# One window loop on one core: constants padded to 128 rows, masks turned in a strip bank, and another order of the TensorE blocks in a slot

## Chip, cores and metric

One NeuronCore of a Trainium2 chip runs the whole program. The metric is the device time of one execution in microseconds (us), taken on that core. The kernel before took 2175.47 us (median of 3 runs, 2175.24 to 2191.92).

## What is computed

For each of 128 batches of 128 nodes with 512 features, the reference makes a self feature, two directions of masked attention against the first 20 nodes with 16 heads, and adds both through a relu to the input:

```python
q_exp = jnp.where(row_zero[..., None], 0.0, q[:, None, :])
self_feat = jnp.concatenate([exp_v, q_exp], axis=-1) @ W_self.T + b_self
output = self_feat
for d in range(2):
    A = (adj_f if d == 0 else jnp.swapaxes(adj_f, 1, 2))[:, :, :20, :]
    qh = (self_feat @ Wq[d].T + bq[d]).reshape(B, N, 16, 32)
    kh = (self_feat[:, :20] @ Wk[d].T + bk[d]).reshape(B, 20, 16, 32)
    aff = einsum('bnhd,bmhd->bnhm', qh, kh) / sqrt(32)
    aff = where((A.sum(-1) > 0)[:, :, None, :], aff, NEG) + (A @ w_bias + b_bias)[:, :, None, :]
    w = softmax(aff)
    out_t = einsum('bnhm,bmf->bnhf', w, self_feat[:, :20])
    output = output + einsum('bnhf,hgf->bnhg', out_t, Wout[d]).reshape(B, N, F) + bout[d]
return exp_v + relu(output)
```

## The kernel before

The program has three stages. Weights are prepared, then keys and values of the 20 nodes of all batches are made and stored in DRAM (k_dram, v_dram), and from about 360 us on the window loop runs, which is where the change lies. It is written engine by engine, by hand: each engine executes its own list strictly in order, and semaphores tie the lists together. No scheduler moves anything.

The window loop works on pairs of batches, 64 of them, one new pair a slot. Slots 0 to 3 and the last ones are written out; the 14 rounds between run in a hardware loop of 4 slots. A pair stays in the window for 4 slots, at ages 0 to 3, and each slot makes one quarter of the scores of all 4 pairs in the window (one direction, 8 heads). In slot t, "soft" is the pair of age 3, whose scores become complete in this slot and whose softmax starts, "late" is the pair before it, "nxt" the pair that enters next. Two batches of a pair are b = 0 and 1.

The parts of a slot that matter here:

- generate(nxt, step), lines 1530 to 1548: makes the operand of the next slot's scores in four banks (low_banks), in 5 steps. Each step is 8 matmuls on strips of 32 rows, four of them side by side. Step 0 makes the constants from zl (line 1545), whose stationary operand has ZR = 41 columns; steps 1 to 4 make the keys (line 1547). All steps write the same columns, so each step waits until the one before it has been copied out. Step 0 is read twice: ScalarE copies it to zc (constants_high, line 1423), then VectorE forms the low part from the same bank (constants_low, line 1255), and step 1 waits for that (z_low). Steps 2 to 4 wait for ScalarE's keys_out (line 1428).
- scores(t, age), lines 1552 to 1569: per batch four float32 matmuls against kx (line 1567) and one fp32r matmul of 41 rows, flags against zc (line 1568), which adds the constants. A float32 matmul is two instructions in the trace, an fp32r matmul one. Two banks take turns, so scores wait for the add_masks of the scores two before (s_added).
- self_features (line 1580), 12 fp32r matmuls of 512 columns per batch into the bank OUT; values (line 1601) adds the attention output there. The next batch's self_features must wait until VectorE has taken OUT away (take_out, line 1294, out_taken).
- turn_weights (line 1593) turns a batch's softmax weights in the bank TURN, and ScalarE copies them out (weights_out, line 1441). TURN also takes flag_rows (line 1609, stationary 128 rows by 41 columns) and, every second slot, turn_mask (line 1615), the turned mask of a group of 4 batches.
- VectorE in a slot: add_masks(t,3) (line 1268), two maxima (line 1280), constants_low(nxt), add_masks(t,2), denominators of batch 0 (lines 1285, 1287), take_out(late,1), denominators of batch 1, add_masks(t,1), the turn of x, count_and_weigh of the edges, add_masks(t,0), total_and_mask, take_out(soft,0).
- GpSimd subtracts the maxima (shift, line 1358) and makes the normalised weights (line 1367); ScalarE makes the exponentials between them (line 1433).
- ScalarE in a slot: clip, high, constants_high(nxt), weights_out(late,1,0), high, exponentials(soft,0), weights_out(late,1,1), keys_out 0, exponentials(soft,1), clip(late,1), two scale_condition, row_sums, keys_out 1, the weights_out of soft's batch 0, and the rest. The masks are copied out of TURN to m1s (line 1460) and placed pair by pair (line 1471).

The order of a slot on TensorE is the code of slot(t):

```python
scores(t, 3); generate(nxt, 0); turn_weights(late, 1, 0)
scores(t, 2); turn_weights(late, 1, 1); generate(nxt, 1); values(late, 1)
scores(t, 1); generate(nxt, 2)
self_features(soft, 0, range(0, 2)); turn_weights(soft, 0, 0)
self_features(soft, 0, range(2, C)); turn_weights(soft, 0, 1)
generate(nxt, 3); scores(t, 0); flag_rows(nxt); values(soft, 0)
generate(nxt, 4); self_features(soft, 1, range(0, C))
# every second slot: turn_mask(g)
```

Of the kernel before, what the change touches and what calls it, by code (L numbers as in the profile page):

```python
# [893 lines left out]
def window_loop(nc, sb, sem, bank, low_banks, v):  # L894
# [28 lines left out]
    zl = sb("zl", [P, NO, ZR], F32)  # L923
    nzm = sb("nzm", [P, WIN, ZR], BF16)
# [11 lines left out]
    m1s = sb("m1s", [P, EDGE, NG], F32)  # L936
# [39 lines left out]
    m1_ready = sem("m1_ready")  # L976
# [19 lines left out]
    OUT, TURN = bank[6], bank[7]  # L996

# [190 lines left out]
    def vector_program(dve):  # L1188
# [18 lines left out]
        def nonzero_rows(p):  # L1207
# [6 lines left out]
            for o in (0, Q):  # L1214
                a = p.ring * (ZR + 1) + o
                nc.vector.tensor_scalar(spread[:, a:a + ZR + 2:ZR + 1], sums[:], 0.0, None,
                                        ALU.not_equal).then_inc(nz_ready, 1)
# [12 lines left out]
        def total_and_mask(g, d):  # L1230
# [6 lines left out]
            if d == 0:  # L1237

                if due(g):
                    dve.wait_ge(mask_set, 4 * g)  # L1240
# [16 lines left out]
        def add_masks(t, a):  # L1257
# [4 lines left out]
            if a == 0:  # L1262
# [3 lines left out]
                dve.wait_ge(mask_set, 2 * (p.n + 1))  # L1266
# [29 lines left out]
        def slot(t):  # L1296
# [28 lines left out]
            if has_edges(g):  # L1325
                count_and_weigh(g, t.c % 2)
            if t.real():
# [3 lines left out]
            if soft.real():  # L1331
                take_out(soft, 0)
# [64 lines left out]
    def scalar_program(act):  # L1397
# [53 lines left out]
        def flags_out(p):  # L1451
            act.wait_ge(pe_e, p.n + 1)
            nc.scalar.activation(flags[0:ZR, p.ring:p.ring + 2, :], TURN[0:ZR, 0:2 * N].rearrange("p (b n) -> p b n", b=2),
                                 ACT.Copy).then_inc(e_out, 1)

        def mask_out(g):
            if due(g):
                act.wait_ge(mask_set, 4 * g)
            act.wait_ge(pe_m1, g + 1)
            nc.scalar.activation(m1s[:].rearrange("p b m -> p (b m)"), TURN[:, 0:EDGE * NG], ACT.Copy).then_inc(m1_ready, 1)  # L1460

        def place_masks(t, p):

            g = edge_group(t.back(1) if p.c % 2 == 0 else t.back(2))
            o = 2 * (p.c % 2)
            if p.back(4).real():
                act.wait_ge(s_added, scored(t, 3))
            act.wait_ge(m_done[0], g + 1)
            act.wait_ge(m1_ready, g + 1)
            for d, m in enumerate((m0s, m1s)):  # L1470
                nc.scalar.activation(masks[:, d, p.ring:p.ring + 2, :], m[:, o:o + 2, :], ACT.Copy).then_inc(mask_set, 1)

        def slot(t):
# [12 lines left out]
            if t.c % 2 == 0 and nxt.real():  # L1486
                place_masks(t, nxt)
# [11 lines left out]
            if nxt.real():  # L1499
                row_sums(nxt)  # L1500
            if has_window(nxt):
# [199 lines left out]
```

## Time and profile before

| what | value |
|---|---|
| median of 3 runs | 2175.47 us |
| the profiled execution, its own time | 2179.28 us |
| its span in the trace | 2177.4 us |
| window loop, from its first matmul to the end | about 364 to 2177 us |
| one slot of the hardware loop | 26.4 to 27.0 us, the first of a round 26.6, 28.2 or once 30.8 us, the last of a round 28.6 to 30.6 us |
| busy share of TensorE, VectorE, ScalarE, GpSimd | 94%, 50%, 48%, 33% |

A row of the trace's groups gives line, engine, tiles, shapes, the count, the busy time and the mean, and behind the second bar the idle time just before and who ended it. PE is TensorE's matmul side, PEld its weight loads, DVE is VectorE, ACT ScalarE, POOL GpSimd, SP SyncE. A weight load that starts well ahead of its own matmul is hidden beside the matmul before; one that starts together with its matmul is not. In a timeline, rows of one line that follow each other are merged, so "1.25 ... x8" is eight matmuls from the first start to the last end; the last end overlaps the next start, and what a block occupies is best read from start to start.

### The profile page before, as it was taken

The numbers are of one execution on the slowest core, as the hardware profiler recorded it, in microseconds if no ns is written. First come the engines' busy times: TensorE is split into PE (matmuls) and PEld (weight loads), VectorE is DVE, ScalarE is ACT, GpSimd is POOL, SyncE is SP. The second block draws the span as 40 slices with busy tenths as digits, with TensorE's granted clock in tenths as the row PEclk, the third lists the DMA queues.
The fourth block names the chain that finished last, engine by engine and source line by source line (L and its number), as shares of the span: only waits on it lengthen the run. The fifth ranks groups of instructions, "written<-read, shape, count | busy, mean of one in ns | idle before, by whom it ended". The sixth has DMA issues, their size and how long they took to land. (4 is left out here: it accounts for less than half of the span.)

```text
span 2177.4 us, 47943 instructions
## 1 busy us (share of the span) xinstructions
PE 2047.9 (94%) x15864; PEld 1708.9 (78%) x15864; DVE 1096.0 (50%) x1937; ACT 1035.0 (48%) x1813; POOL 725.2 (33%) x617
## 2 busy tenths in 40 slices
PE   8999997799999999999999999999999999999997
PEld 5999996677777777777777777777777777777786
DVE  3433333455555555555555555555555545555532
ACT  3323232355455555555555555555555545455543
POOL 0323220033333333333333333333333333333334
PEclk9999998799999999999999999999999999999998
DMA  6132334444354435443444444444443444444322
GB/s 199 35 95 87 91 101 113 124 130 127 113 135 130 128 109 134 120 126 117 127 114 130 119 137 116 138 112 139 114 134 109 131 120 126 126 126 127 100 72 73
DMA packets 263777, 256.08 MB, mean 118 GB/s; under 512 B 78192, under 2 KB 194160, under 8 KB 263536
## 3 DMA queue, kind: packets, MB, share of 16 engines
q1 hardware_dynamic: 259072, 252.83, 41.5%
q8 instruction: 153, 2.51, 0.5%
q10 hardware_dynamic: 4464, 0.02, 0.1%
q14 instruction: 88, 0.72, 0.1%
HBM read 197.94 MB, written 54.79 MB: 116 GB/s over the span
## 5 line engine op out<-in xcount | busy, mean ns | idle before, releaser
L1567 PE MATMUL bank<-kx,xt_main 128*128 128x160 f32 x4096 | 691.2, 312 | 29.7 <-issue 29.4
L1567 PEld LDWEIGHTS bank<-kx,xt_main 128*128 128x128 f32 x4096 | 586.1, 193 | 73.5 <-issue 44.9
L1268 DVE TENSOR_TENSOR sc<-bank,masks 128x320 f32<-128x320 f32 x256 | 125.8, 492 | 712.8 <-PE bank L1568 712.8
L1376 POOL TENSOR_TENSOR res<-res,xk 128x512 f32<-128x512 f32 x128 | 163.5, 1277 | 879.5 <-ACT res L1418 879.5
L1428 ACT ACTIVATE kx<-low_banks 128x1280 f32<-128x1280 f32 (+3 forms) x268 | 317.9, 1186 | 182.8 <-PE low_banks L1547 182.7
L1580 PE MATMUL bank<-ws_h,xh_main 128*128 128x512 f32 x512 | 221.8, 433 | 52.4 <-DVE res L1294 52.3
L1547 PE MATMUL low_banks<-key_tile,a_rows 32*128 32x160 f32 (+3 forms) x4288 | 221.6, 321 | 17.6 <-DVE zc L1255 12.1
L1358 POOL TENSOR_TENSOR sc<-sc,mx 128x640 f32<-128x640 f32 x128 | 160.1, 1272 | 176.0 <-DVE mx L1280 175.9
L1423 ACT ACTIVATE zc<-low_banks 41x1280 fp32r<-41x1280 f32 (+2 forms) x67 | 79.3, 1184 | 265.3 <-PE low_banks L1545 265.3
L1580 PE MATMUL bank<-ws_h,xl_main 128*128 128x512 f32 x512 | 203.1, 397 | 0.0
L1580 PE MATMUL bank<-ws_l,xh_main 128*128 128x512 f32 x512 | 202.8, 396 | 0.0
L1547 PEld LDWEIGHTS low_banks<-key_tile,a_rows 32*128 32x128 f32 x4288 | 158.7, 188 | 54.3 <-issue 20.9
L1441 ACT ACTIVATE wtt<-bank 128x384 f32<-128x384 f32 (+1 forms) x256 | 110.9, 433 | 181.4 <-PE bank L1593 181.3
L1352 POOL TENSOR_TENSOR xl_main<-xt_main,xh_main 128x512 fp32r<-128x512 f32 x128 | 162.7, 1271 | 65.9 <-ACT xh_main L1407 65.9
L1601 PE MATMUL bank<-vbd,wtt 128*128 128x128 f32 x1280 | 177.7, 286 | 3.6 <-ACT wtt L1441 3.5
L1367 POOL TENSOR_TENSOR wt<-sc,rs 128x640 f32<-128x640 f32 x128 | 163.1, 1274 | 45.4 <-DVE rs L1287 45.4
L1568 PE MATMUL bank<-zc,flags 41*128 41x160 f32 x512 | 175.4, 343 | 0.0
L1601 PEld LDWEIGHTS bank<-vbd,wtt 128*128 128x128 f32 x1280 | 153.5, 192 | 21.1 <-ACT wtt L1441 9.6
L1580 PEld LDWEIGHTS bank<-ws_h,xh_main 128*128 128x128 f32 x512 | 96.4, 188 | 92.9 <-issue 70.8
L1568 PEld LDWEIGHTS bank<-zc,flags 41*128 41x128 f32 x512 | 94.6, 185 | 89.6 <-issue 89.6
L75 DVE STREAM_TRANSPOSE xt_main<-rows_main 128x256 f32<-128x256 f32 x256 | 141.6, 608 | 0.0
L1294 DVE TENSOR_TENSOR res<-bank,res 128x512 f32<-128x512 f32 x128 | 87.9, 687 | 83.6 <-PE bank L1601 83.6
(145 smaller groups left out, 3095.7 us busy)
## 6 DMA issues: line engine op xcount, KB each, us to landing
rows_main<-in_x SPq DMA_DIRECT2D x256, 128.0 KB, 4.6
xs<-in_x SPq DMA_DIRECT2D x64, 512.0 KB, 4.8
xk<-in_x SPq DMA_DIRECT2D x64, 512.0 KB, 3.9
res<-c_dram SPq DMA_DIRECT2D x64, 512.0 KB, 5.8
out<-res SPq DMA_DIRECT2D x128, 256.0 KB, 2.2
adj<-in_mask_BxSxSx_ik SPq DMA_DIRECT2D x32, 440.0 KB, 7.0
adj<-in_mask_BxSxSx_ik SPq DMA_DIRECT2D x128, 110.0 KB
vbd<-v_dram SPq DMA_DIRECT2D x768, 10.0 KB
```

What stands on the lines that cost most here:

```text
L75: return eng.transpose(dst, src.rearrange("p t (r j) -> p t r j", j=NQ)[:, :, :, j])
L1268: nc.vector.tensor_tensor(o[:, :, HU * hh:HU * hh + HU, d, :], s_bank(t, a).rearrange("p (b h m) -> p b h m", b=2, m=NG), masks[:, d, p.ri ...
L1352: pool.tensor_tensor(xl[:, :, b, :], xt[:, :, p.ring + b, :], xh[:, :, b, :].bitcast(F32), ALU.subtract).then_inc(x_low, 1)
L1358: pool.tensor_tensor(s, s, mx[:, b, :].unsqueeze(2).to_broadcast([P, DIRS * H, NG]), ALU.subtract).then_inc(s_shifted, 1)
L1367: pool.tensor_tensor(wt[:, b, :].rearrange("p (h m) -> p h m", m=NG), sc[:, p.ring + b, :].rearrange("p (h m) -> p h m", m=NG), rs[:, b, : ...
L1376: pool.tensor_tensor(res[:, p.par, b, :], res[:, p.par, b, :], xk[:, p.par, b, :], ALU.add).then_inc(res_ready, 1)
L1428: nc.scalar.activation(taken(kx[:, t.par, j], lo, hi), generated(0, P, lo, hi), ACT.Copy).then_inc(gen_taken, 1)
L1547: mm = nc.tensor.matmul(low_banks[:, r, dst], a_rows[s, o, step - 1, :], rhs, start=True, stop=True)
L1567: mm = nc.tensor.matmul(dst, xt[:, j, p.ring + b, :], kx[:, t.par, j, :, :, w, :].rearrange("p r c m -> p c r m"), start=(j == 0), stop=False)
L1568: mm = nc.tensor.matmul(dst, flags[0:ZR, p.ring + b, :], zc[0:ZR, t.par, :, :, w, :].rearrange("p r c m -> p c r m"), start=False, stop=True)
L1580: mm = nc.tensor.matmul(OUT[:], a, m[:, j, :], start=(j == 0 and k == 0), stop=False)
L1601: mm = nc.tensor.matmul(OUT[:, 3 * c * DH:(3 * c + SLOTS) * DH], wtt[:, b, c, :], vbd[:, p.par, c, :, b * DH:b * DH + DH], start=False, st ...
```

## The change

It has three parts.

First, padding: ZR is no longer used for zl, nzm, zc and flags in the window loop. They are 128 wide, zero beyond row 40, so that the constants' stationary operand has 32 rows by 128 columns, flag_rows 128 by 128, and the last matmul of each batch's scores 128 rows.

Second, masks: the turned mask of a group goes to unused columns of the first strip bank (MASK) instead of TURN, in the middle of an even slot. The copy m1s is gone; the masks are placed once a group for 4 batches, behind row_sums in ScalarE's list, and generate(nxt, 3) waits for that.

Third, order: TensorE's slot begins with generate(nxt, 0) and turn_weights(late, 1, 0), ahead of scores(t, 3); scores(t, 2) stands behind values(late, 1); scores(t, 0) stands behind values(soft, 0). VectorE's take_out(soft, 0) stands ahead of add_masks(t, 0). The rest of VectorE's list is as it was. Line numbers after the change are lower by 1 to 15.

```diff
-    zl = sb("zl", [P, NO, ZR], F32)
-    nzm = sb("nzm", [P, WIN, ZR], BF16)
+    zl = sb("zl", [P, NO, P], F32)
+    nzm = sb("nzm", [P, WIN, P], BF16)
...
+    MASK = low_banks[:, 0, 2 * UN:2 * UN + EDGE * NG]
...
             if d == 0:
 
                 if due(g):
-                    dve.wait_ge(mask_set, 4 * g)
+                    dve.wait_ge(mask_set, 2 * g)
...
-                dve.wait_ge(mask_set, 2 * (p.n + 1))
+                dve.wait_ge(mask_set, 2 * (p.half + 1))
...
                 count_and_weigh(g, t.c % 2)
+            if soft.real():
+                take_out(soft, 0)
             if t.real():
                 add_masks(t, 0)
             if has_edges(g):
                 total_and_mask(g, t.c % 2)
-            if soft.real():
-                take_out(soft, 0)
...
-            nc.scalar.activation(taken(zc[0:ZR, t.par], lo, hi), generated(0, ZR, lo, hi), ACT.Copy).then_inc(z_high, 1)
+            nc.scalar.activation(taken(zc[:, t.par], lo, hi), generated(0, P, lo, hi), ACT.Copy).then_inc(z_high, 1)
...
-        def place_masks(t, p):
...
+        def place_masks(t):
+
+            if t.back(3).real():
                 act.wait_ge(s_added, scored(t, 3))
-            act.wait_ge(m_done[0], g + 1)
-            act.wait_ge(m1_ready, g + 1)
-            for d, m in enumerate((m0s, m1s)):
-                nc.scalar.activation(masks[:, d, p.ring:p.ring + 2, :], m[:, o:o + 2, :], ACT.Copy).then_inc(mask_set, 1)
+            act.wait_ge(m_done[0], t.half + 1)
+            act.wait_ge(pe_gen, STEPS * (t.n + 1) + 3)
+            for d, m in enumerate((m0s[:], MASK.rearrange("p (b m) -> p b m", b=EDGE))):
+                nc.scalar.activation(masks[:, d, t.ring:t.ring + EDGE, :], m, ACT.Copy).then_inc(mask_set, 1)
...
-                        mm = nc.tensor.matmul(low_banks[0:ZR, r, dst], zl[s, o, :], rhs, start=True, stop=True)
+                        mm = nc.tensor.matmul(low_banks[:, r, dst], zl[s, o, :], rhs, start=True, stop=True)
...
-                mm = nc.tensor.matmul(dst, flags[0:ZR, p.ring + b, :], zc[0:ZR, t.par, :, :, w, :].rearrange("p r c m -> p c r m"), start=False, stop=True)
+                mm = nc.tensor.matmul(dst, flags[:, p.ring + b, :], zc[:, t.par, :, :, w, :].rearrange("p r c m -> p c r m"), start=False, stop=True)
...
-                mm = nc.tensor.matmul(TURN[0:ZR, b * N:b * N + N], nzm[:, p.ring + b, :], identity_b[:],
+                mm = nc.tensor.matmul(TURN[:, b * N:b * N + N], nzm[:, p.ring + b, :], identity_b[:],
...
-            if soft.real():
-                scores(t, 3)
             if has_window(nxt):
                 generate(nxt, 0)
             if late.real():
 
                 pe.wait_ge(e_out, t.n + 1 if t.real() else PAIRS)
-                g = edge_group(t.back(2) if t.c % 2 == 0 else t.back(3))
-                pe.wait_ge(m1_ready, g + 1 if has_edges(g) else EG)
                 turn_weights(late, 1, 0)
-            if t.back(2).real():
-                scores(t, 2)
+            if soft.real():
+                scores(t, 3)
             if late.real():
                 turn_weights(late, 1, 1)
             if has_window(nxt):
                 generate(nxt, 1)
             if late.real():
                 values(late, 1)
+            if t.back(2).real():
+                scores(t, 2)
             if t.back(1).real():
                 scores(t, 1)
+            if t.c % 2 == 0 and t.real():
+                turn_mask(t)
             if has_window(nxt):
                 generate(nxt, 2)
...
             if has_window(nxt):
+                if t.c % 2 == 0 and t.real():
+                    pe.wait_ge(mask_set, 2 * (t.half + 1))
                 generate(nxt, 3)
-            if t.real():
-                scores(t, 0)
...
             if soft.real():
                 values(soft, 0)
+            if t.real():
+                scores(t, 0)
             if has_window(nxt):
                 generate(nxt, 4)
             if soft.real():
                 self_features(soft, 1, range(0, C))
-            if t.c % 2 == 1:
-                g = edge_group(t.back(1))
-                if has_edges(g):
-                    if nxt.real():
-                        pe.wait_ge(e_out, nxt.n + 1)
-                    turn_mask(g)
```

On TensorE, in the first slot of the hardware loop, this stood from turn_weights(late, 1, 0) to the wait of generate(nxt, 1) before the change (z_low is raised by VectorE's constants_low; line 1567 and 1568 are scores(t, 2)):

```order
L1593 MATMUL bank<-identity,wt 128x128 [waits wt_ready,wtt_ready,m1_ready,e_out]
L1593 MATMUL bank<-identity,wt 128x128 x2
L1560 REGISTER_ALU
L1567 MATMUL bank<-kx,xt_main 128x160 [waits s_added]
L1567 MATMUL bank<-kx,xt_main 128x160 x3
L1568 MATMUL bank<-zc,flags 128x160
L1567 MATMUL bank<-kx,xt_main 128x160 x4
L1568 MATMUL bank<-zc,flags 128x160
L1588 REGISTER_ALU [waits wt_ready]
L1593 MATMUL bank<-identity,wt 128x128 [waits wtt_ready]
L1593 MATMUL bank<-identity,wt 128x128
L1547 MATMUL low_banks<-key_tile,a_rows 128x160 [waits z_low]
```

Scores(t, 3) had stood above generate(nxt, 0), so that the whole of scores(t, 2) lay between scores(t, 3) and the wait for z_low. In the changed kernel, from the end of scores(t, 3) on (lines 1552, 1553), the same stretch reads:

```order
L1552 MATMUL bank<-kx,xt_main 128x160 [waits gen_taken]
L1553 MATMUL bank<-zc,flags 128x160
L1552 MATMUL bank<-kx,xt_main 128x160 x4
L1553 MATMUL bank<-zc,flags 128x160
L1573 REGISTER_ALU [waits wt_ready]
L1578 MATMUL bank<-identity,wt 128x128 [waits wtt_ready]
L1578 MATMUL bank<-identity,wt 128x128
L1532 MATMUL low_banks<-key_tile,a_rows 128x160 [waits z_low]
L1532 MATMUL low_banks<-key_tile,a_rows 128x160 x7
L1584 REGISTER_ALU [waits vbd_loaded1]
L1586 MATMUL bank<-vbd,wtt 128x128 [waits wtt_ready]
L1586 MATMUL bank<-vbd,wtt 128x128 x4
```

Between scores(t, 3) and the wait for z_low now stand two transposes.

On VectorE the slot begins as it did: this is the changed kernel, and before it was the same with lines one higher (the ISA and REGISTER rows between carry no work):

```order
L1267 TENSOR_TENSOR sc<-bank,masks 128x2x8x20 [waits pe_s]
L1279 TENSOR_REDUCE mx<-sc 128x32 [waits s_added] x2
L1251 REGISTER_ALU
L1254 TENSOR_TENSOR zc<-low_banks,zc 9x1280 [waits z_high]
L1260 REGISTER_ALU
L1267 TENSOR_TENSOR sc<-bank,masks 128x2x8x20 [waits pe_s]
```

constants_low (line 1254) keeps its place behind add_masks of scores(t, 3) and both maxima. At the end of VectorE's slot, before the change:

```order
L1227 TENSOR_TENSOR adj<-adj,wb 128x880 [waits edge_sum]
L1261 REGISTER_ALU
L1268 TENSOR_TENSOR sc<-bank,masks 128x2x8x20 [waits mask_set,wt_ready,pe_s]
L1233 TENSOR_REDUCE vb<-adj 128x80 [waits weighed]
L1234 TENSOR_SCALAR mk<-cn 128x80
L1240 REGISTER_ALU [waits masked,bias_sum0]
L1247 SCALAR_TENSOR_TENSOR m0s<-vb,bb,mk 128x80 [waits mask_set]
L1294 TENSOR_TENSOR res<-bank,res 128x512 [waits pe_out,c_scaled]
```

and in the changed kernel, where take_out (line 1293) has moved ahead of add_masks and of the mask's arithmetic:

```order
L1226 TENSOR_TENSOR adj<-adj,wb 128x880 [waits edge_sum]
L1293 TENSOR_TENSOR res<-bank,res 128x512 [waits pe_out,c_scaled]
L1260 REGISTER_ALU
L1267 TENSOR_TENSOR sc<-bank,masks 128x2x8x20 [waits mask_set,wt_ready,pe_s]
L1232 TENSOR_REDUCE vb<-adj 128x80 [waits weighed]
L1233 TENSOR_SCALAR mk<-cn 128x80
L1246 SCALAR_TENSOR_TENSOR m0s<-vb,bb,mk 128x80 [waits mask_set,masked,bias_sum0]
```

TensorE's self_features(soft, 1) waits for that take_out, and in the changed kernel scores(t, 0) and generate(nxt, 4) stand between the values that it needs and that wait.

## Rows read from the trace of the kernel before

**Rows 1.** The page: busy time of each engine, share of the span, instructions.

```profile
PE 2047.9 (94%) x15864; PEld 1708.9 (78%) x15864; DVE 1096.0 (50%) x1937; ACT 1035.0 (48%) x1813; POOL 725.2 (33%) x617
```

**Rows 2.** Who waited for whom, whole span: total us, times, longest.

```profile
PEld bank L1568 <- issue: 89.6, 512, 0.3
...
PE bank L1580 <- DVE res L1294: 52.3, 65, 1.1
...
PE bank L1567 <- issue: 29.4, 13, 3.5
```

**Rows 3.** Timeline of the start of one slot (start us, length us, engine).

```profile
1034.82 1.24 PEld L1567 LDWEIGHTS bank<-kx,xt_main 128*128 128x128 f32 x8
1035.04 1.25 PE L1567 MATMUL bank<-kx,xt_main 128*128 128x160 f32 x8
...
1036.22 0.18 PEld L1568 LDWEIGHTS bank<-zc,flags 41*128 41x128 f32 x1 [0.17 <-issue]
1036.22 0.34 PE L1568 MATMUL bank<-zc,flags 41*128 41x160 f32 x1
...
1036.49 1.35 PE L1567 MATMUL bank<-kx,xt_main 128*128 128x160 f32 x8
...
1038.05 0.75 PE L1545 MATMUL low_banks<-key_tile,zl 32*41 32x160 f32 x16
1038.15 0.49 DVE L1268 TENSOR_TENSOR sc<-bank,masks 128x320 f32<-128x320 f32 x1 [6.14 <-PE bank L1568]
1038.68 1.54 DVE L1280 TENSOR_REDUCE mx<-sc 128x32 f32<-128x640 f32 x2
...
1039.58 2.50 POOL L1358 TENSOR_TENSOR sc<-sc,mx 128x640 f32<-128x640 f32 x2 [3.69 <-DVE mx L1280]
...
1040.25 1.48 DVE L1255 TENSOR_TENSOR zc<-low_banks,zc 9x1280 fp32r<-9x1280 f32 x1
...
1042.12 0.44 PE L1593 MATMUL bank<-identity,wt 128*128 128x128 f32 x2
...
1042.49 0.83 PE L1547 MATMUL low_banks<-key_tile,a_rows 32*128 32x160 f32 x16
```

**Rows 4.** The windows of that slot's four scores: sum of lengths, then PE busy.

```profile
sum 12.13, PE 12.13 PEld 10.06 DVE 5.55 ACT 6.53 POOL 5.50; mean PE 3.03 PEld 2.51 DVE 1.39 ACT 1.63 POOL 1.37
```

**Rows 5.** Timeline of the middle of that slot, one engine after the other.

```profile
1044.73 0.69 DVE L1294 TENSOR_TENSOR res<-bank,res 128x512 f32<-128x512 f32 x1 [0.90 <-PE bank L1601]
...
1045.46 0.63 ACT L1418 ACTIVATE res<-res 128x512 f32<-128x512 f32 x1 [0.21 <-DVE res L1294]
...
1048.45 1.22 ACT L1428 ACTIVATE kx<-low_banks 128x1280 f32<-128x1280 f32 x1
1050.31 0.49 ACT L1441 ACTIVATE wtt<-bank 128x384 f32<-128x384 f32 x1 [0.64 <-PE bank L1593]
...
1047.47 0.83 PE L1547 MATMUL low_banks<-key_tile,a_rows 32*128 32x160 f32 x16
...
1051.46 0.38 PE L1593 MATMUL bank<-identity,wt 128*128 128x128 f32 x2
```

**Rows 6.** TensorE's first matmuls behind three loop boundaries, with the gap.

```profile
1555.90 1.35 PE L1567 MATMUL bank<-kx,xt_main 128*128 128x160 f32 x8 [2.53 <-issue]
...
1777.62 2.50 PE L1567 MATMUL bank<-kx,xt_main 128*128 128x160 f32 x8 [3.46 <-issue]
...
1891.83 1.84 PE L1567 MATMUL bank<-kx,xt_main 128*128 128x160 f32 x8 [2.83 <-issue]
```

**Rows 7.** Windows of first slots of a round: length, busy times, granted clock, DMA.

```profile
1006.80:1035.00 28.20, 27.48 (x208) 22.37 (x209) 14.35 (x27) 14.23 (x24) 10.72 (x10) 0.94 0.41 120
...
1227.90:1254.50 26.60, 25.93 (x209) 21.11 (x210) 14.34 (x27) 14.45 (x25) 11.58 (x10) 1.00 0.42 121
...
1777.60:1808.40 30.80, 30.11 (x208) 24.57 (x209) 14.35 (x27) 14.23 (x24) 9.83 (x9) 0.85 0.36 104
```

**Rows 8.** The values block (line 1601), full shapes in a row.

```profile
1055.85 1.38 PE L1601 MATMUL bank<-vbd,wtt 128*128 128x128 f32 x10
```

More of the change, by code:

```diff
@@ L975, in window_loop @@
     pe_m1 = sem("pe_m1")
-    m1_ready = sem("m1_ready")
     mask_set = sem("mask_set")
@@ L1214, in nonzero_rows @@
             for o in (0, Q):
-                a = p.ring * (ZR + 1) + o
-                nc.vector.tensor_scalar(spread[:, a:a + ZR + 2:ZR + 1], sums[:], 0.0, None,
+                a = p.ring * (P + 1) + o
+                nc.vector.tensor_scalar(spread[:, a:a + P + 2:P + 1], sums[:], 0.0, None,
                                         ALU.not_equal).then_inc(nz_ready, 1)
@@ L1485, in slot @@
                 exponentials(soft, 0)
-            if t.c % 2 == 0 and nxt.real():
-                place_masks(t, nxt)
             if late.real():
@@ L1500, in slot @@
                 row_sums(nxt)
+            if t.c % 2 == 0 and t.real():
+                place_masks(t)
             if has_window(nxt):
@@ L1511, in slot @@
                 keys_out(nxt, 3)
-            if t.c % 2 == 1:
-                g = edge_group(t.back(1))
-                if has_edges(g):
-                    mask_out(g)
-                if nxt.real():
-                    place_masks(t, nxt)
         slots(act, slot, -2)
@@ L1608, in flag_rows, with turn_mask @@
             for b in range(2):
-                mm = nc.tensor.matmul(TURN[0:ZR, b * N:b * N + N], nzm[:, p.ring + b, :], identity_b[:],
+                mm = nc.tensor.matmul(TURN[:, b * N:b * N + N], nzm[:, p.ring + b, :], identity_b[:],
                                       start=True, stop=True)
             mm.then_inc(pe_e, 1)
-        def turn_mask(g):
-            pe.wait_ge(m_done[1], g + 1)
-            nc.tensor.transpose(TURN[:, 0:EDGE * NG], m1r[:], identity[0:EDGE * NG, 0:EDGE * NG]).then_inc(pe_m1, 1)
+        def turn_mask(t):
+            pe.wait_ge(gen_taken, C * (t.n + 1) + 1)
+            pe.wait_ge(m_done[1], t.half + 1)
+            nc.tensor.transpose(MASK, m1r[:], identity[0:EDGE * NG, 0:EDGE * NG]).then_inc(pe_m1, 1)
         def slot(t):
             soft, late, nxt = t.back(3), t.back(4), t.back(-1)
-            if soft.real():
-                scores(t, 3)
             if has_window(nxt):
@@ L1646, in slot @@
             if has_window(nxt):
+                if t.c % 2 == 0 and t.real():
+                    pe.wait_ge(mask_set, 2 * (t.half + 1))
                 generate(nxt, 3)
-            if t.real():
-                scores(t, 0)
             if nxt.real():
@@ L1653, in slot @@
                     pe.wait_ge(wtt_ready, 2 * (2 * soft.n + 1))
-                else:
-                    g = edge_group(t.back(2) if t.c % 2 == 0 else t.back(3))
-                    if due(nxt.n):
-                        pe.wait_ge(e_out, nxt.n)
-                    if due(g + 1):
-                        pe.wait_ge(m1_ready, g + 1)
+                elif due(nxt.n):
+                    pe.wait_ge(e_out, nxt.n)
                 flag_rows(nxt)
@@ L1666, in slot @@
                 self_features(soft, 1, range(0, C))
-            if t.c % 2 == 1:
-                g = edge_group(t.back(1))
-                if has_edges(g):
-                    if nxt.real():
-                        pe.wait_ge(e_out, nxt.n + 1)
-                    turn_mask(g)
         slots(pe, slot, -2)
```

11 lines of the change are left out of this document (1 added, 10 removed).

## The prediction

> **What bounds the kernel now.** I read the page first: TensorE is busy 94% of the span, the next engine 50% [rows 1]. So the time is TensorE's list plus the places where it stands still. The waits come next [rows 2]. TensorE waits 52.3 us in all for VectorE's take_out ahead of self_features (65 times, at most 1.1), and 29.4 us over 13 loop boundaries. The third line is no wait for anyone: ahead of each of the 512 loads of line 1568 the weight-load side idles, 89.6 us in all. The timeline of one slot shows what that is [rows 3]. The eight loads of line 1567 start 0.22 us ahead of their matmuls and stay ahead, so they are hidden. The load of line 1568, with 41 rows, starts together with its matmul at 1036.22, so it is not hidden, and the next load of 128 rows is not either. So TensorE is at its limit, but part of its busy time is exposed weight loading. Everything else must be read as a question of who is late when TensorE's order changes.
>
> **Part 1, padding.** The period of line 1567: eight matmuls take 1.25 us, the last is 0.30 long, so (1.25 - 0.30)/7 = 0.136. With a steady period the matmul of line 1568 would start 8 x 0.136 = 1.09 behind the first; it starts at 1.18 (1036.22 - 1035.04). From there to the next start is 0.27, and the following eight take 1.35 in place of 1.25. Where full shapes follow each other there is no such loss, and the type is not the cause: the loads of line 1567 (float32) at 1034.82 run under the last matmul of line 1580 (fp32r), which gives way at 1035.04 [rows 3]. What follows an fp32r matmul of 160 columns can start once its own weights are in. Ten matmuls of line 1601, of 128 columns, take 1.38 with their first load exposed, a period of at most 0.12 [rows 8]; I take 0.11. With 128 rows I price a batch's scores at 8 x 0.136 + 0.11 = 1.20, a pair's at 2.40, four at 9.6, plus 0.1 because two of them are followed or preceded by strips. Now they take 12.13 a slot [rows 4]. That is -2.4 a slot, over 64 slots -155 us. The bounds: nothing gained if the load stays exposed, -155 if all is hidden; I take the latter, because the full-shaped neighbours in these rows are hidden.
>
> A rule that speaks against it stands in the Trainium skill, TensorE: Matmul & The Clock Gate, Part 3 (The mechanism): weight loads overlap running matmuls only where the row groups differ. By it a padded load, which shares all its rows with its neighbours, would stay exposed. The trace disagrees for line 1567 [rows 3], whose loads are on the same 128 rows and run 0.22 us ahead; by the rule the sum would be 155 us higher.
>
> The smaller changes of shape: the constants' strips cost what the key strips cost (0.75 start to start in place of 0.68), the slot's end now passes from full shapes to strips (about +0.1), and in return the flag rows, the values behind them and the two transposes lose their own exposed loads (about -0.3). These are small differences of start times within a block; the sum is -0.1 a slot, -6 us, between -20 and +6. The larger one-time clears on VectorE I leave at nothing.
>
> **Part 2, the masks.** Off TensorE this removes a copy and half of the placings on ScalarE, 48% busy; on TensorE one short transpose moves from the slot's end to its middle. The new waits are light: the strip bank's columns are free, the mask of a group is finished a slot earlier, and all of self_features(soft, 0) lies between generate 2, behind which ScalarE places, and generate(nxt, 3). I cost it at 0, between -5 (two start-up waits for the mask) and +6 us (0.1 a slot). In even slots the two copies stand ahead of keys_out 1, which counts below.
>
> **Part 3, the order.** The gain: take_out(soft,0) no longer stands behind the mask's arithmetic, and scores(t,0) and generate 4 (3.2 us together) stand between values(soft,0) and self_features(soft,1). The wait of 52.3 us [rows 2] goes whole; nothing else is late there, since ScalarE's last keys_out (1.2) still ends under the 2.9 us of self_features.
>
> The price lies at the front of the slot. Generate(nxt,1) may not start before constants_low. VectorE reaches constants_low only behind add_masks of scores(t,3) and both maxima, and none of that moved. Before: scores(t,3) gives way at 1038.05, VectorE works 0.49, 1.54 and 1.48 and ends at 1041.73, that is 3.68 later; TensorE comes to generate 1 at 1042.49, 4.44 later, so it hid this with 0.7 to spare [rows 3]. It hid it under generate 0 (0.68), a transposing block (0.39), scores(t,2) (3.00) and another (0.37). Of these only the last, now 0.31, stands there afterwards. So TensorE waits 3.68 + 0.1 (semaphore) - 0.31 = 3.45 us in each slot. A second gate ends at nearly the same time: values(late,1), right behind generate 1, needs weights_out(late,1,1), which on ScalarE stands behind exponentials(soft,0), which needs the first shift (GpSimd starts it 1.5 us after scores(t,3) gives way and takes half of 2.50 [rows 3]). That is ready while generate 1 runs, so it adds nothing, but it would keep most of the wait if constants_low were early. 63 slots have both blocks: 63 x 3.45 = +217 us. Behind the waiting matmul stands the whole list of TensorE, and everyone waits for that.
>
> A second new wait: scores(t,2) now ends late. From its end VectorE needs add_masks, denominators and take_out(late,1): before, take_out ended at 1045.42, that is 3.3 behind scores(t,2) at 1042.12, of which 0.90 was idle, so 2.4. Then ScalarE clips; from clip to keys_out 1 is 2.99 us and to the following weights_out at least 1.1 [rows 5], plus 0.49 and two semaphores of some 0.1. That is 7.2 after scores(t,2). TensorE, with scores(t,1) 2.45 and what lies from generate 2 to turn_weights(soft,0,1), 1051.46 - 1047.47 = 3.99 [rows 5], comes there after 6.4. So 0.8 a slot, x 62 = +50. Bounds: 0 if ScalarE is a little faster, 1.1 (+68) with the masks' copies.
>
> So far: -155 - 6 - 52 + 217 + 50 = +54 us.
>
> **The clock.** In the loop TensorE stands still at each of 13 boundaries, 2.3 us on average, 3.5 at most [rows 2]. After seven of them the granted clock falls from 2.4 to 1.2 GHz: the window rows show 0.94 and a first slot of 28.2 us in six, and once 0.85 and 30.8 us, against 26.6 us at 1.00 in the others [rows 7]. The two longest gaps, 2.83 and 3.46 us, were followed by a fall, the longest by the long one; one of 2.53 was not, and its eight matmuls took their usual 1.35 [rows 6]. The new wait is 3.45 us, in every slot. I therefore let the clock fall in nearly every slot. The price of one fall is 1.6 us, once 4.2; the mean of the seven is (6 x 1.6 + 4.2)/7 = 1.97. I take 1.9, since a few waits may go without: 63 x 1.9 = +120 us. The bounds are 0 and 4.2 a slot (+265). The slow stretch comes right behind the wait, on generate, values and scores(t,2), all on the path.
>
> **Sum.** 2179.3 (the profiled execution; its span is 2177.4) + 54 + 120 = 2353. The median of the runs is 3.8 lower, so 2350. A slot would be about 29.7 us in place of 27.
>
> **Rivals.**
> (a) The wait comes, the clock stays up. Place and sum as above without the last term: 2230 us. For it: six of 13 boundary gaps left the clock alone. Against: the longer gaps did not [rows 6], and this wait is 3.45.
> (b) Padding buys nothing, the exposed load only changes its rows. Then 155 us more: 2505 us. For it: line 1568's load and the one behind it share rows with their neighbours and are exposed. Against: the loads of line 1567 share all rows with theirs, behind lines 1567 and 1580 alike, and are hidden [rows 3].
> (c) The other side, faster. The place is the wait of generate(nxt,1). If it is no wait (the maxima and constants_low finish under what TensorE has to do), the gains of 155 + 6 + 52 stand alone: 1962 us. With the clock up, the wait decides at about 2.5 us a slot: with the 0.8 of the second wait that eats the 3.35 of gains. For it: VectorE idles 6.14 us ahead of add_masks, so it is never behind on anything old. Against: three instructions whose lengths hardly vary, 3.51 us of work in series behind scores(t,3), and only two transposes to cover them.
> (d) It comes out even: the wait near 3.3, the second wait hidden, no fall: 2175 us plus or minus 20.
>
> **Chances.** The forecast 0.66 (own range 2290 to 2440), (a) 0.14, (b) 0.06, (c) 0.08, (d) 0.06. A measurement of this kernel can tell about 1% from no change. Faster by over 1%: 0.08, all (c). Within 1%: 0.06. Slower: 0.86. The range leaves out (b), (c) and most of (d): 2190 to 2450, from (a) with the second wait hidden (2230 - 50 = 2180, nearly) to the forecast with falls that cost 3.5 us each (2230 + 63 x 3.5 = 2450).
>
> **What would show it.** In the profile afterwards, the wait list should have a new line: TensorE, low_banks of line 1532, waiting for VectorE's zc of line 1254 (or for ScalarE's kx or wtt), about 217 us over some 63 times, longest 3.5. The wait for take_out should be gone and the idle loads ahead of line 1553 too; one scores block should take 2.4 us at full clock. A slot's window should show a granted clock of about 0.85 to 0.94 nearly everywhere, and the whole span about 0.9. The second wait stands at line 1578 for ScalarE's wtt, about 0.8 each. The prediction is wrong if the strips' wait is under 2.5 us, if scores still take 3.0, or if the mean granted clock stays at 0.98, each by the size of its own term.

## The result and the profile after

| what | before | after |
|---|---|---|
| median of 4 runs | 2179.97 us (2175.24 to 2191.92) | 2344.46 us (2319.77 to 2349.53) |
| ratio, 95% interval | | 1.0723 [1.0632, 1.0814] |
| profiled execution: its time, its span | 2179.28, 2177.4 us | 2348.28, 2346.5 us |
| mean granted clock of the span | 0.981 | 0.917 |
| one slot of the hardware loop, most of them | 26.4 to 27.0 us | 29.1 to 31.2 us |

The kernel became 7.2% slower; 2350 us had been forecast. The page of the kernel after, to be held against [rows 1]:

```profile
span 2346.5 us, 47654 instructions
...
PE 2032.0 (87%) x15864; PEld 1795.2 (77%) x15864; DVE 1085.4 (46%) x1937; ACT 1001.8 (43%) x1717; POOL 724.4 (31%) x617
...
PEclk9999997999999998898988898999888999999998
```

TensorE's share fell from 94% to 87% with the same number of instructions. Its busy time hardly changed, 2047.9 to 2032.0, and that is not one fact but two that cancel: matmuls at the lower clock count as longer. The clock row has eights all through the loop.

Its waits, as in [rows 2] (total us, times, longest), first of the whole span, then of the loop alone, from 430 us on:

```profile
PE bank L1578 <- ACT wtt L1440: 29.5, 60, 0.7
...
PE low_banks L1530 <- issue: 15.2, 13, 2.6
...
PE bank L1565 <- DVE res L1293: 3.9, 5, 1.7
```

```profile
PE low_banks L1532 <- DVE zc L1254: 216.2, 63, 3.7
```

The wait of generate(nxt, 1) for z_low is there 63 times and costs 216.2 us. The second wait stands at turn_weights (line 1578) for weights_out. The wait for take_out has gone from 52.3 to 3.9 us, and the 13 loop boundaries from 29.4 to 15.2. The line "PEld bank L1568 <- issue: 89.6" of [rows 2] has no successor; the loads of the last matmul of a batch's scores now have nothing idle ahead of them (the last figure of the group):

```profile
L1553 PEld LDWEIGHTS bank<-zc,flags 128*128 128x128 f32 x512 | 104.6, 204 | 0.0
```

The timeline of a slot's start answers to [rows 3] (start us, length us, engine):

```profile
1027.45 0.83 PE L1530 MATMUL low_banks<-key_tile,zl 32*128 32x160 f32 x16
...
1028.59 1.25 PE L1552 MATMUL bank<-kx,xt_main 128*128 128x160 f32 x8
...
1029.54 0.19 PEld L1553 LDWEIGHTS bank<-zc,flags 128*128 128x128 f32 x1
1029.57 0.34 PE L1553 MATMUL bank<-zc,flags 128*128 128x160 f32 x1
...
1029.75 1.29 PE L1552 MATMUL bank<-kx,xt_main 128*128 128x160 f32 x8
...
1030.95 0.38 PE L1578 MATMUL bank<-identity,wt 128*128 128x128 f32 x2
...
1031.15 0.49 DVE L1267 TENSOR_TENSOR sc<-bank,masks 128x320 f32<-128x320 f32 x1 [5.38 <-PE bank L1553]
1031.67 1.55 DVE L1279 TENSOR_REDUCE mx<-sc 128x32 f32<-128x640 f32 x2
1033.25 1.48 DVE L1254 TENSOR_TENSOR zc<-low_banks,zc 9x1280 fp32r<-9x1280 f32 x1
...
1034.52 0.37 ACT L1440 ACTIVATE wtt<-bank 128x256 f32<-128x256 f32 x1
...
1034.79 0.82 PE L1532 MATMUL low_banks<-key_tile,a_rows 32*128 32x160 f32 x16 [3.46 <-DVE zc L1254]
1035.55 1.95 PE L1586 MATMUL bank<-vbd,wtt 128*128 128x128 f32 x10
1037.28 2.34 PE L1552 MATMUL bank<-kx,xt_main 128*128 128x160 f32 x8
...
1040.79 1.28 PE L1552 MATMUL bank<-kx,xt_main 128*128 128x160 f32 x8
...
1043.28 0.83 PE L1532 MATMUL low_banks<-key_tile,a_rows 32*128 32x160 f32 x16
...
1047.80 0.44 PE L1578 MATMUL bank<-identity,wt 128*128 128x128 f32 x2 [0.37 <-ACT wtt L1440]
```

Scores(t,3) give way at 1030.95. VectorE then works 0.49, 1.55 and 1.48 us in series and ends at 1034.73; TensorE resumes at 1034.79 after 3.46 us of idleness. ScalarE's weights_out(late,1,1), the second gate, ends at 1034.89, only 0.1 later. Behind the standstill the same eight matmuls that take 1.28 us at 1040.79 take 2.34 (at 1037.28), and ten of line 1586 take 1.95 where [rows 8] had 1.38: that is the clock. At full clock the scores of one pair take 2.49 us (1040.79 to 1043.28), where they took 3.01 before (1035.04 to 1038.05 in [rows 3]).

Three neighbouring slots as windows, as in [rows 7] (length, busy times of PE, PEld, DVE, ACT, POOL, granted clock, DMA):

```profile
1150.30:1180.20 29.90, 25.27 (x213) 21.96 (x212) 15.87 (x27) 13.76 (x22) 10.77 (x10) 0.94 0.41 113
1180.20:1210.50 30.30, 26.26 (x213) 22.88 (x213) 14.18 (x27) 14.04 (x24) 9.23 (x8) 0.89 0.39 121
1210.50:1240.80 30.30, 26.46 (x213) 23.02 (x212) 15.87 (x27) 13.76 (x22) 9.92 (x9) 0.89 0.37 112
```

Before, most slots had 1.00. Now 60 of 62 whole slots of the loop have a fall.

### The profile page after: what moved, and what is told of

Read it like the earlier page. It is cut to its first block, busy times and chain, and to the rows that moved or that the text cites. A ratio compares the mean times of both kernels' runs of the same rounds, so it can differ in the third digit from the quotient of the medians.

```text
span 2346.5 us, 47654 instructions
## 1 busy us (share of the span) xinstructions
PE 2032.0 (87%) x15864; PEld 1795.2 (77%) x15864; DVE 1085.4 (46%) x1937; ACT 1001.8 (43%) x1717; POOL 724.4 (31%) x617
## 4 chain that ended last, share of the span: by engine, by line
PE 66%; DVE 13%; ACT 11%; issue 6%; ACTq 0%; DMA 0%; DVEq 0%; POOL 0%; POOLq 0%; SPq 0%
PE bank L1552 21%; PE bank L1586 9%; PE bank L1565 9%; PE low_banks L827 8%; PE low_banks L1532 8%; DVE zc L1254 4%; PE bank L827 4%; ACT kx L1427 3%; ACT xs L1448 3%; ACT res L1411 3%; DVE mx L1279 3%; PE bank L1578 3%; PE low_banks L1530 2%; DVE sm L1284 2%; DVE res L1293 2%
## 5 line engine op out<-in xcount | busy, mean ns | idle before, releaser
L1552 PEld LDWEIGHTS bank<-kx,xt_main 128*128 128x128 f32 x4096 | 640.1, 209 | 0.9 <-issue 0.8
L1532 PE MATMUL low_banks<-key_tile,a_rows 32*128 32x160 f32 (+3 forms) x4288 | 250.1, 353 | 236.5 <-DVE zc L1254 231.0
L1532 PEld LDWEIGHTS low_banks<-key_tile,a_rows 32*128 32x128 f32 x4288 | 179.8, 211 | 278.0 <-DVE zc L1254 246.7
L1586 PE MATMUL bank<-vbd,wtt 128*128 128x128 f32 x1280 | 232.6, 345 | 5.2 <-ACT wtt L1440 5.1
L1417 ACT ACTIVATE res<-res 128x512 f32<-128x512 f32 x128 | 80.1, 625 | 366.6 <-DVE res L1293 366.6
L1586 PEld LDWEIGHTS bank<-vbd,wtt 128*128 128x128 f32 x1280 | 205.2, 247 | 24.6 <-issue 23.3
L1432 ACT ACTIVATE sc<-sc 128x640 f32<-128x640 f32 x128 | 93.7, 732 | 223.7 <-POOL sc L1357 223.7
L1553 PE MATMUL bank<-zc,flags 128*128 128x160 f32 x512 | 186.3, 364 | 0.0
L1578 PE MATMUL bank<-identity,wt 128*128 128x128 f32 x640 | 119.1, 284 | 29.5 <-ACT wtt L1440 29.5
L1578 PEld LDWEIGHTS bank<-identity,wt 128*128 128x128 f32 x640 | 72.7, 141 | 75.8 <-ACT wtt L1440 51.3
```

What stands on the lines that cost most here:

```text
L1532: mm = nc.tensor.matmul(low_banks[:, r, dst], a_rows[s, o, step - 1, :], rhs, start=True, stop=True)
L1552: mm = nc.tensor.matmul(dst, xt[:, j, p.ring + b, :], kx[:, t.par, j, :, :, w, :].rearrange("p r c m -> p c r m"), start=(j == 0), stop=False)
L1553: mm = nc.tensor.matmul(dst, flags[:, p.ring + b, :], zc[:, t.par, :, :, w, :].rearrange("p r c m -> p c r m"), start=False, stop=True)
L1578: mm = nc.tensor.transpose(TURN[:, (c - lo) * P:(c - lo) * P + P], wt[:, b, c * P:c * P + P], identity[:])
L1586: mm = nc.tensor.matmul(OUT[:, 3 * c * DH:(3 * c + SLOTS) * DH], wtt[:, b, c, :], vbd[:, p.par, c, :, b * DH:b * DH + DH], start=False, st ...
```

## Where the 169 us come from

The two spans differ by 169.1 us (the medians by 164.5). I split that from 430 us on, into TensorE's idle time, and its busy time as it would be at full clock; what is over is the price of the lower clock (half of the busy time spent at 1.2 GHz). These three sums are counted from the trace's single records.

| part | before | after | difference |
|---|---|---|---|
| busy, as at full clock | 1636 | 1482 | -154 |
| price of the lower clock | 19 | 158 | +139 |
| idle | 87 | 271 | +184 |

The idle part by the wait lists: 216.2 for z_low, 29.5 second wait, 52.3 - 3.9 = 48.4 less for take_out, 29.4 - 15.2 = 14.2 less at the boundaries; together 183.

## Experiments

Eight kernels, in two groups of four that ran on one chip each. The kernel before, in the same groups, took 2179.0 and 2187.1 us; ratios are against it. Each number of a kernel is the median of 4 runs.

**pad_only: the kernel before with the padding alone.**

```diff
-    zl = sb("zl", [P, NO, ZR], F32)
-    nzm = sb("nzm", [P, WIN, ZR], BF16)
+    zl = sb("zl", [P, NO, P], F32)
+    nzm = sb("nzm", [P, WIN, P], BF16)
...
-                mm = nc.tensor.matmul(dst, flags[0:ZR, p.ring + b, :], zc[0:ZR, t.par, :, :, w, :].rearrange("p r c m -> p c r m"), start=False, stop=True)
+                mm = nc.tensor.matmul(dst, flags[:, p.ring + b, :], zc[:, t.par, :, :, w, :].rearrange("p r c m -> p c r m"), start=False, stop=True)
```

> The kernel before with the padding alone: zl, nzm, zc and flags 128 wide, masks and order as they were. Theory (padding hides the weight loads of the constants' matmuls, 2.5 us a slot): 64 x 2.5 = 160 us less than before, about 2015 us, four scores of a slot 9.7 us in place of 12.1, the idle weight-load side ahead of line 1568 gone, clock as before. Rival (the load stays exposed and padding buys nothing): 2175 us, scores still 12.1.

Measured: 2052.17 us, ratio 0.9418 [0.9380, 0.9456]. The padding pays, so the rival by which a padded load stays exposed is out. The four scores of a slot at full clock went from 12.2 to 9.7 us (mean of the single records, start to next start). But the kernel gained 127 us, not 160. Two rows of its waits, whole span:

```profile
PE bank L1580 <- DVE res L1294: 66.2, 65, 1.3
...
PE bank L1567 <- issue: 37.3, 13, 3.6
```

Busy time at full clock fell by 159 us, as forecast. Of that, 14 us came back as a longer wait for take_out (52.3 to 66.2), because TensorE arrives earlier at a VectorE that is no faster; 8 at the loop boundaries (29.4 to 37.3), and 7 as lower clock.

**no_pad: the change without its padding.**

```diff
-    zl = sb("zl", [P, NO, P], F32)
-    nzm = sb("nzm", [P, WIN, P], BF16)
+    zl = sb("zl", [P, NO, ZR], F32)
+    nzm = sb("nzm", [P, WIN, ZR], BF16)
```

and the flags, zc and matmuls likewise.

> The changed kernel with the constants back at 41 rows and columns, order and masks as changed. Theory: the exposed loads come back, 2.5 us a slot, the wait for z_low stays 3.46: 2344 + 160 = about 2500 us. Rival (in the changed order the longer scores fall partly into waits and the padding is worth less than there): 2344 to 2450 us.

Measured: 2420.67 us, ratio 1.1102 [1.1057, 1.1148]. That is the rival's range and not the 2500 us of the theory: inside the change the padding is worth 76 us, half of its work. Two of its waits, one of the matmul side and one of the load side:

```profile
PE low_banks L1532 <- DVE zc L1254: 222.3, 67, 8.1
...
PEld bank L1553 <- issue: 90.6, 512, 0.3
```

The exposed loads are back. But the wait for z_low is 9 us shorter than after (231.0 over the same 67), the second wait of 29.5 us is down to 0.7, since scores(t,1) stands ahead of it and takes 0.6 us longer, the boundaries cost 7.7 in place of 15.2, and the lower clock costs 123 in place of 158 us. The spans differ by 70: 150 of work, less 35 of clock and 45 of idle time. Why the lower clock costs less behind nearly the same standstill (3.31 us, a fall behind 61 of 62) no run shows.

**filler: does the standstill alone lower the clock?** On the kernel after, 11 matmuls of 128 rows by 160 columns stand ahead of the wait. They write columns that nobody reads and add work that the computation doesn't need.

```diff
+                if soft.real() and t.back(2).real():
+                    pe.wait_ge(s_added, scored(t, 2) - 2)
+                    for _ in range(11):
+                        nc.tensor.matmul(s_bank_full(t, 2)[:, 2 * UN:2 * UN + 160], identity[:],
+                                         a_rows[:, 0, 0:2, :].rearrange("p c q -> p (c q)")[:, 0:160],
+                                         start=True, stop=True)
                 generate(nxt, 1)
```

> The changed kernel with 11 float32 matmuls of 160 columns (0.27 us each, 3.0 in all) into unused columns of a score bank, ahead of the wait for z_low; they are added work whose result nobody reads. The wait ends when it did, but TensorE is busy in it. Theory (the granted clock falls because of the 3.46 us standstill, and costs about 120 us): the clock stays near 1.00 in most slots and the time is about 2230 us. Rival (the clock costs little, the loss is waits alone): no faster than the changed kernel, 2344 us. A third outcome, slower than 2344, would say that the filler itself is on the path.

Measured: 2217.97 us, ratio 1.0166 [1.0123, 1.0210], mean clock 0.985. The path at the front is as long as without the filler, with 0.47 us of wait left a slot (its waits, whole span; 26.6 of the 41.3 us lie in the loop):

```profile
PE low_banks L1536 <- DVE zc L1254: 41.3, 61, 7.7
```

Two of 62 slots have a fall, both right behind a loop boundary, and the time is 126 us lower, by work that does nothing. So the clock's price is shown, and rival (a), 2230, is about what the kernel would be with the clock up. Its size is known less well: by the two ratios it is 121 us, with some 22 us either way. In the profiled executions, split as in the table, the lower clock's price falls from 158 to 8 us and 18 come back, 8 of them at the boundaries and nearly all the rest as work, since the filler is 9 us more than the wait that it takes away.

**filler5: the same with 5 such matmuls**, so that 2.1 us of standstill are left.

```diff
-                    for _ in range(11):
+                    for _ in range(5):
```

> The filler run with 5 matmuls in place of 11: 1.4 us of the wait are filled, some 2.1 us of standstill are left in every slot. Theory (the clock answers to the length of the standstill, and falls after some standstills of 1.5 to 2.5 us, as at the loop boundaries of the kernel before): falls in about half of the slots, 2218 + 63 x 0.5 x 1.6 = about 2270 us, mean clock about 0.96. Rivals: every slot still falls (2340 us), or none does (2218 us).

Measured: 2248.89 us, ratio 1.0300 [1.0258, 1.0343]. Two neighbouring slots, neither of them the first of a round, as windows, and then the wait in each:

```profile
1180.48:1207.89 27.41, 24.93 (x220) 21.65 (x219) 15.87 (x27) 13.75 (x22) 9.92 (x9) 1.00 0.43 125
1207.89:1237.14 29.25, 26.57 (x220) 23.36 (x219) 14.17 (x27) 14.03 (x24) 10.07 (x9) 0.94 0.38 114
```

```profile
1187.83 0.82 PE L1536 MATMUL low_banks<-key_tile,a_rows 32*128 32x160 f32 x16 [2.10 <-DVE zc L1254]
...
1215.23 0.83 PE L1536 MATMUL low_banks<-key_tile,a_rows 32*128 32x160 f32 x16 [2.10 <-DVE zc L1254]
```

TensorE stands still for 2.10 us in both, once without a fall and once with one. 20 of 62 slots have a fall, a third, not the half that I had expected. And only 15 of the 62 standstills have one behind them; 8 falls came right behind a loop boundary, 3 of them in slots that had both.

**low_first: constants_low ahead of VectorE's add_masks and maxima.** This takes away only the first gate.

```diff
+            if has_window(nxt):
+                constants_low(nxt)
             if soft.real():
...
                 maxima(t, 1)
-            if has_window(nxt):
-                constants_low(nxt)
             if t.back(2).real():
```

> The changed kernel with constants_low moved to the start of VectorE's slot, ahead of add_masks 3 and the maxima. Theory of two gates (the values right behind generate 1 wait for ScalarE's copy of the turned weights, which stands behind the exponentials of soft's batch 0, and these behind the maxima and GpSimd's shift): the wait moves from generate 1 to the values and is 2.9 us in place of 3.5, a slot 0.6 shorter, the clock falls still: about 2300 us. Rival (z_low is the only gate): the wait is gone and the time is under 2020 us.

Measured: 2261.30 us, ratio 1.0351 [1.0302, 1.0400]. The standstill moved from generate(nxt, 1) to values(late, 1), first in its waits, then in the timeline of one slot:

```profile
PE bank L1586 <- ACT wtt L1440: 182.7, 65, 3.7
```

```profile
1033.09 1.48 DVE L1254 TENSOR_TENSOR zc<-low_banks,zc 9x1280 fp32r<-9x1280 f32 x1 [3.80 <-ACT zc L1422]
...
1034.74 0.83 PE L1532 MATMUL low_banks<-key_tile,a_rows 32*128 32x160 f32 x16
...
1037.36 0.74 ACT L1432 ACTIVATE sc<-sc 128x640 f32<-128x640 f32 x1 [3.41 <-POOL sc L1357]
...
1038.01 0.36 ACT L1440 ACTIVATE wtt<-bank 128x256 f32<-128x256 f32 x1
...
1038.42 2.50 PE L1586 MATMUL bank<-vbd,wtt 128*128 128x128 f32 x10 [2.85 <-ACT wtt L1440]
```

Constants_low is early and generate(nxt, 1) starts at once. Then values wait 2.85 us for a copy of 0.36 that stands behind exponentials(soft,0), which waits for GpSimd, which waits for the maxima. 45 of 62 slots have a fall, 42 of them behind this standstill and 3 at a boundary. Against the kernel after, the profiled span is 90 us shorter: 39 of idle time, which was forecast, and 54 of lower clock, which was not; that is why it came out under the 2300 us expected.

**both_first: low_first, and ScalarE's weights_out(late,1,1) ahead of exponentials(soft,0).**

```diff
                 high(soft, 1)
-                exponentials(soft, 0)
             if late.real():
                 weights_out(late, 1, 1)
+            if soft.real():
+                exponentials(soft, 0)
```

> As low_first, and on ScalarE weights_out(late,1,1) ahead of exponentials(soft,0), so that both gates of the front are lifted while TensorE keeps its changed order. Theory (the order itself is harmless once nothing behind the maxima is needed): no wait over 0.5 us at the front, the second wait of 0.4 to 0.6 us at the turns of soft's batch 0 remains, clock near 1.00: 1945 + 63 x 0.6 = about 1985 us. Rival (a third gate, such as the late denominators or the second wait growing): over 2050 us.

Measured: 1992.17 us, ratio 0.9123 [0.9085, 0.9161]. With both gates open the order of the change is 9% faster than the kernel before. (ScalarE's gate alone was not opened in any run.) Its waits show what is left, the second wait and the boundaries:

```profile
PE bank L1579 <- ACT wtt L1440: 29.7, 60, 0.7
...
PE low_banks L1531 <- issue: 21.7, 13, 2.9
```

**old_front: the change with the first half of the slot in its old order**, that is padding, masks, and the later place of scores(t,0) and earlier one of take_out.

```diff
+            if soft.real():
+                scores(t, 3)
             if has_window(nxt):
...
-            if soft.real():
-                scores(t, 3)
+            if t.back(2).real():
+                scores(t, 2)
             if late.real():
...
                 values(late, 1)
-            if t.back(2).real():
-                scores(t, 2)
```

> The changed kernel with the old front of TensorE's slot: scores 3, constants' strips, late turns, scores 2, then generate 1 and the values; padding, masks, take_out and scores 0 behind the values stay changed. Theory (all of the loss comes from taking scores 2 away from in front of generate 1): no wait for z_low, no second wait at the turns of soft's batch 0, no wait for take_out, a slot of about 24 us, 1960 us in all. Rival (the masks or the late scores 0 carry part of the loss): the wait for z_low goes but the time stays over 2015 us, the time expected of the padding alone.

Measured: 1945.12 us, ratio 0.8915 [0.8879, 0.8951], the best of all, 15 us under what I expected. The window of a slot shows TensorE busy all through it, and its waits the boundaries:

```profile
1024.70:1048.00 23.30, 23.30 (x209) 20.65 (x210) 14.46 (x27) 14.05 (x24) 8.43 (x8) 1.00 0.43 124
```

```profile
PE bank L1552 <- issue: 20.7, 13, 2.7
```

In the loop only 29 us of idle time are left, most of it at the boundaries; in it the wait for take_out is down to 2.5 us and the second wait to 1.5. The whole loss of the change, 399 us against this kernel, lies in the order of the slot's first half.

**pad_mask: the kernel before with padding and the new way of the masks**, in the old order everywhere. Its edit is the change without the third part; of it, on TensorE:

```diff
-        def turn_mask(g):
-            pe.wait_ge(m_done[1], g + 1)
-            nc.tensor.transpose(TURN[:, 0:EDGE * NG], m1r[:], identity[0:EDGE * NG, 0:EDGE * NG]).then_inc(pe_m1, 1)
+        def turn_mask(t):
+            pe.wait_ge(gen_taken, C * (t.n + 1) + 1)
+            pe.wait_ge(m_done[1], t.half + 1)
+            nc.tensor.transpose(MASK, m1r[:], identity[0:EDGE * NG, 0:EDGE * NG]).then_inc(pe_m1, 1)
```

> The kernel before with padding and the masks' new way, its order of blocks and of VectorE as before. Theory (the masks' part is worth nothing, between -5 and +6 us): 2052 plus or minus 6, with the wait for take_out at 66 us as with the padding alone. Rival (taking the mask's transpose away from the end of every second slot, where the loop boundary's gap follows, changes that gap or the falls of the clock behind it): 2025 us or less, with shorter gaps. From this kernel to old_front (1945) only take_out and the late scores 0 differ: 66 us of wait and what hangs on it.

Measured: 2039.82 us, ratio 0.9339 [0.9303, 0.9375]. Between the two groups only ratios compare well: 0.9418 with the padding alone. That is 17 us, with some 11 us either way. The profiled spans, 2047.7 and 2037.9, are 10 us apart. So the masks, which I had put at 0, are worth some 10 to 17 us. Its waits:

```profile
PE bank L1565 <- DVE res L1293: 63.2, 65, 1.3
...
PE bank L1552 <- issue: 36.6, 13, 3.6
```

By the split of the table, 5 of the 10 us are lower clock (21 in place of 26; 11 slots with a fall in place of 13), 3 are in the wait for take_out, and 1 each in the other idle time and in TensorE's work. The falls differ from one execution to the next, so half of the gain rests on a term that is not steady. From here to old_front it is 95 us: the later scores(t,0) and earlier take_out remove 61 of the 63 us of waits, and with them go 16 at the boundaries, 14 of lower clock and 5 of work.

## Why the prediction was right, point by point

The mechanism and its place held: two transposes can't cover what constants_low needs, TensorE stands still behind them in every slot, and the clock falls. The sum of +174 us met +169 between the spans. That it came so close is partly luck: the clock cost 19 us more than forecast and two smaller gains than forecast cost 7 and 4, while the second wait was 20 us shorter and the boundaries gave 14 back.

- Padding and shapes, -161: measured -159 alone and -154 inside the change (there with what the masks' part does to TensorE's work). The bound at "nothing gained" (rival (b), 2505) is excluded by pad_only. The split within a batch was not as I drew it: the matmul of line 1553 starts 0.03 us behind the last of line 1552 and the next batch's first 0.18 us behind that (1029.57 and 1029.75), where I had put 0.136 and 0.11. A whole batch takes 1.16 to 1.20, a pair 2.37 in most cases (the one shown above 2.49), where I had 1.20 and 2.40. The rule of the Trainium skill that weight loads overlap only where the row groups differ (TensorE: Matmul & The Clock Gate, The mechanism), taken alone, would have left the gain at nothing; pad_only, 127 us faster, disagrees with it for these loads. The same section also names the background weight buffer as a case in which a load is pulled ahead; whether these loads use it, no run shows.
- Masks, 0: measured -10 to -17, with the uncertainty given above. The term was outside its own bounds of -5 to +6, though not by much. I had looked only for what the new waits might cost, not for what the clock and take_out might give back.
- Take_out, -52: measured -48.4. It went with the later place of scores(t,0), as argued; pad_mask keeps it, old_front does not.
- The wait for z_low, 63 x 3.45 = +217: measured 216.2, 3.46 in the slot shown. The lengths of VectorE's three instructions were read off the old timeline and did not change by more than 0.01 us. Around them smaller errors cancel: VectorE started 0.20 us after scores(t,3) gave way, not 0.10, while the way from its end to TensorE took 0.06, not 0.1, and the transposes covered 0.38, not 0.31. (The three terms as the text has them add up to 3.47, not 3.45.) The second gate behind it was where the text put it: low_first moves the standstill there and keeps 2.85 of 3.46 us.
- The second wait, +50: measured 29.5. This is the largest error among the waits. From the end of scores(t,2) to weights_out's release I had 7.2 us and it took 7.0 (1040.79 to 1047.80); TensorE was to come after 6.4 and came after 6.6. The wait is a small difference between two long paths: 0.2 us on each turns 0.8 into 0.4.
- The boundaries: not in the sum. They gave 14.2 us back.
- The clock, 63 x 1.9 = +120: measured +139 in the profiled executions, and 126 between medians by filler. The low clock comes in stretches of one length, or two or three of them end to end. The price of one stretch was right: in the 62 whole slots of the loop 94 stretches cost 149 of the 158 us, 1.6 each, as I had read. What I missed is their number: 28 slots have one stretch, 30 have two and 2 have three. The executions of the kernel after lie 30 us apart (2319.77 to 2349.53, mean clock 0.928 and 0.917): the falls are not the same in each execution.

Rival (c), faster, needed constants_low to be early. low_first shows that this alone was not enough: ScalarE's copy had to be early too, as the prediction's text on the second gate had it, and then (both_first) the kernel is faster indeed, 1992 us where (c) said 1962. The second wait, 29.7 us, which (c) left out, is about as large as the difference; other terms moved too.

## What to carry to other kernels

Before a consumer is moved up, follow everything that it needs through the lists of the engines that make it: here a gain of 160 us on TensorE was spent by a slot order in which two short operations of other engines (1.48 and 0.36 us) stood behind some 2 and 3 us of work and waiting for things that TensorE didn't need yet. Opening the first gate of two that end 0.1 us apart bought 83 us (2344 to 2261), opening both 352 (1992), nearly as much as the old order of the front (399). And a standstill of TensorE was paid twice here, once as idle time and once in the clock of the matmuls behind it: 216 and about 126 us.

## What the runs showed of the hardware

The clock after a standstill. I count a fall as following a standstill when the lower clock begins in it or within 2.5 us behind it. In the 62 whole slots of the loop, in kernels whose slots differ only by the edits above, a standstill of 3.46 us was followed by a fall 60 times (the kernel after), one of 2.85 us 42 times (low_first), one of about 2.1 us 15 times (filler5), and one of 0.47 us never (filler). The gaps at the loop boundaries give a second series, in all ten kernels 126 of over 0.3 us:

| length of the gap | gaps | followed by a fall |
|---|---|---|
| 0.3 to 1.5 us | 47 | 0 |
| 1.5 to 2 us | 31 | 11 |
| 2 to 2.5 us | 17 | 13 |
| 2.5 to 3 us | 22 | 19 |
| over 3 us | 9 | 8 |

The chance grows with the length; I had treated it as a yes or no. The length isn't all: at some 2.1 us a boundary was mostly followed by a fall, and the standstill in the middle of TensorE's list mostly not. What decides in a single slot, no run shows.

The gap at the loop's back edge. The trace puts it down to "issue", in which TensorE waits for nothing that it shows. Around the gap of 2.53 us that ends at 1555.90 [rows 6], the DMA view of the kernel before for 1553 to 1556 us has one packet on the queue that fetches instructions:

```profile
q8 instruction: 1, 0.02, 1.9%
```

In the single records of the kernels before and pad_only, all 26 gaps end 2.6 to 2.8 us after the start of such a 16 KB packet, while the gaps themselves were 1.5 to 3.6 us long. In most of the other kernels' gaps it is 2.6 to 3 us too; the kernel after scatters most, 2.7 to 4.5 us. So the gap looks like a fetch of code, shorter where the fetch starts before TensorE has run out. This is read from when things happened and not tested. Why it starts earlier in one kernel than in another (15.2 us over 13 boundaries after, 37.3 in pad_only) stays open; no run was made for it.
